# One-hot matrices of a top-k expert layer, written slot-innermost for experts 2 to 7

## What is computed

```python
logits = xf @ router_w + router_b
scores = jax.nn.softmax(logits, axis=-1)
G, idx = jax.lax.top_k(scores.T, K)            # K = 512 of 2048 tokens, for each of 8 experts
toks = xf[idx]
h1 = jax.nn.relu(jnp.einsum('ekh,ehf->ekf', toks, w1) + b1[:, None, :])
eo = jnp.einsum('ekf,efh->ekh', h1, w2) + b2[:, None, :]
y = jnp.zeros_like(xf).at[idx.reshape(-1)].add((eo * G[..., None]).reshape(-1, h))
```

## Time and profile before

| | |
|---|---|
| median of 3 runs | 611.17 us (611.14 to 612.07) |
| the profiled execution | 611.78 us, of which the span is 609.9 us |
| mean granted PE clock | 0.993 of full speed |
| experts' part of the span | 399 to 603 us |

### The profile page before, as it was taken

The page is one execution under the profiler, slowest core; times in us unless marked ns, Lnnn a source line. Parts: engine busy times, 40 slices in busy tenths (PEclk is TensorE's granted clock), DMA queues, the critical chain, the costliest instruction groups (busy, mean ns, idle before and its releaser), DMA issues.

```text
span 609.9 us, 12823 instructions
## 1 busy us (share of the span) xinstructions
PE 564.1 (92%) x5053; PEld 332.2 (54%) x5053; DVE 435.4 (71%) x797; ACT 397.9 (65%) x771; POOL 194.7 (32%) x192
## 2 busy tenths in 40 slices
PE   5899899989999999999999998899999999999991
PEld 4433333334343343433334444479889898898981
DVE  4789879996889968899894257646765757755620
ACT  1677799977988879898888720054655555646641
POOL 4048030043600335100194020230633625427324
PEclk9999999999999999999999999999999999999997
DMA  8600000001000000000000150012634645346123
GB/s 277 229 1 1 1 1 3 2 1 37 2 35 2 2 36 1 37 1 2 36 35 2 37 172 2 27 46 101 139 103 105 164 123 130 108 105 163 18 25 34
DMA packets 23759, 35.76 MB, mean 59 GB/s; under 512 B 3443, under 2 KB 16148, under 8 KB 23572
## 3 DMA queue, kind: packets, MB, share of 16 engines
q1 hardware_dynamic: 17556, 26.56, 13.2%
q0 software_dynamic: 6144, 8.39, 8.0%
HBM read 26.56 MB, written 8.39 MB: 57 GB/s over the span
## 4 chain that ended last, share of the span: by engine, by line
PE 68%; DVE 17%; ACT 5%; issue 4%; POOL 3%; DMA 1%; SPq 0%; POOLq 0%; ACTq 0%; DVEq 0%
PE ps L1578 15%; PE ps L1571 15%; PE ps L1363 11%; DVE mquart L958 11%; PE ps L1350 6%; PE ps L1329 5%; PE ps L1265 3%; ACT probs L703 2%; PE ps L1241 2%; POOL xn L500 2%; PE ps L1387 1%; PE ps L1405 1%; PE ps L1418 1%; PE ps L1540 1%; PE ps L1549 1%
## 5 line engine op out<-in xcount | busy, mean ns | idle before, releaser
L958 DVE TENSOR_REDUCE mquart<-ps 128x2 f32<-128x802 f32 x256 | 241.7, 987 | 34.4 <-PE ps L1329 31.1
L703 ACT ACTIVATE probs<-ps 128x512 f32<-128x512 f32 (+1 forms) x416 | 222.2, 599 | 23.8 <-PE ps L1350 20.9
L1363 PE MATMUL ps<-probs,vp 128*32 128x256 f32 (+1 forms) x1664 | 132.7, 391 | 4.2 <-ACT osb L612 4.2
L1205 DVE TENSOR_TENSOR h1l<-hf,h1h 128x512 fp32r<-128x512 f32 x64 | 44.1, 690 | 70.7 <-ACT hf L815 70.7
L1329 PE MATMUL ps<-kpad,qrows 64*128 64x401 bf16 x512 | 90.0, 337 | 3.7 <-DVE mquart L958 3.1
L1350 PE MATMUL ps<-qfull,kpad 64*128 64x256 bf16 (+1 forms) x832 | 87.9, 272 | 1.8 <-ACT xf L625 0.6
L814 ACT ACTIVATE h1h<-ps,b1T 128x512 fp32r<-128x512 f32 x64 | 43.9, 686 | 61.1 <-PE ps L1571 60.9
L1578 PE MATMUL ps<-w2h,h1h 128*128 128x256 f32 x256 | 73.8, 288 | 1.4 <-DVE h1l L1205 0.7
L1578 PE MATMUL ps<-w2l,h1h 128*128 128x256 f32 x256 | 72.4, 283 | 0.0
L1578 PE MATMUL ps<-w2h,h1l 128*128 128x256 f32 x256 | 72.3, 283 | 0.0
L582 POOL DMA_INDIRECT out<-eo,idx_put x32 | 54.8, 1713 | 29.6 <-ACT eo L824 20.4
(11 more groups left out here) (175 smaller groups left out, 702.3 us busy)
## 6 DMA issues: line engine op xcount, KB each, us to landing
w1raw<-in_L_ffn_w SPq DMA_DIRECT2D x16, 512.0 KB, 4.3
w2raw<-in_L_ffn_w SPq DMA_DIRECT2D x16, 512.0 KB, 4.6
xs<-in_x SPq DMA_DIRECT2D x4, 512.0 KB, 7.5
ctx_sb<-in_ctx SPq DMA_DIRECT2D x3, 512.0 KB, 5.9
out<-xs SPq DMA_DIRECT2D x3, 512.0 KB, 4.5
x_rows<-x SPq DMA_DIRECT2D x3, 512.0 KB, 2.6
b2b<-in_L_ffn_b SPq DMA_DIRECT2D x1, 1024.0 KB, 11.9
out<-xs SPq DMA_DIRECT2D x2, 256.0 KB, 2.0
```

Source lines behind the costliest of these rows:

```text
L703: nc.scalar.activation(out_p, ps[0:w, next_bank(), :], ACT.Exp, scale=float(SCALE)).then_inc(s_ex, 1)
L958: nc.vector.tensor_reduce(mquart[:, u % 2, t, a, :, kq], ps[:, b:b + 2, 0:MAXW], AX.X, ALU.max).then_inc(s_mr, 1)
L1205: nc.vector.tensor_tensor(h1l[:, f, :], hf[:, f % 2, :], h1h[:, f, :].bitcast(F32), ALU.subtract).then_inc(s_hl, 1)
L1363: last = mm(ps[32 * hh:32 * hh + 32, PV, 0:UW], vp[0:w, kt, g, hh, :], probs[0:w, step % PROBS, hh, :], start=(kt == 0), stop=(kt == NKT - 1))
```

## The change

The tile `onehot` gets a second view, `by_tile` [128 partitions, 16 tokens t, 128 slots r], over the same memory. The one-hots of experts 0 and 1 are written and read as before. Those of experts 2 to 7 are written through `by_tile`: the compare takes `iota_b`, repeated over t, against `pos_row` with each value repeated over 128 slots. `fill_slots` loads `by_tile[:, t, :]`, 128 contiguous bf16, where it loaded `onehot[:, :, t]`, 128 values with a step of 16 elements (32 bytes). The count of instructions, the element counts, the semaphores and the order on every engine stay.

```diff
+FIRST_SLOTS = 2
...
+        by_tile = onehot[:, :, :].rearrange("p r t -> p (r t)").rearrange("p (t r) -> p t r", r=P)
...
-                nc.vector.tensor_tensor(onehot[:, :, a:a + NT], iota_x[:, :, a:a + NT],
-                                        pos_row[:, n:n + NT].unsqueeze(1).to_broadcast([P, P, NT]), ALU.is_equal).then_inc(s_oh, 1)
+                if e < FIRST_SLOTS:
+                    out, row = onehot[:, :, a:a + NT], iota_x[:, :, a:a + NT]
+                    pos = pos_row[:, n:n + NT].unsqueeze(1).to_broadcast([P, P, NT])
+                else:
+                    out, row = by_tile[:, a:a + NT, :], iota_b[:, :].unsqueeze(1).to_broadcast([P, NT, P])
+                    pos = pos_row[:, n:n + NT].unsqueeze(2).to_broadcast([P, NT, P])
+                nc.vector.tensor_tensor(out, row, pos, ALU.is_equal).then_inc(s_oh, 1)
...
-                    last = mm(ps[:, 0, 0:5 * NT], onehot[:, :, t], dat_hit[:, t, :, :].rearrange("p s j -> p (s j)"),
+                    last = mm(ps[:, 0, 0:5 * NT], onehot[:, :, t] if e < FIRST_SLOTS else by_tile[:, t, :], dat_hit[:, t, :, :].rearrange("p s j -> p (s j)"),
```

## The result

| | before | after |
|---|---|---|
| median, runs side by side | 611.61 us (6 runs) | 607.74 us (6 runs) |
| ratio | | 0.994, 95% interval 0.9926 to 0.9954 |
| the profiled execution, its span | 611.78, 609.9 us | 608.77, 606.9 us |
| one expert's period (experts 1 to 5) | 24.94 to 24.96 us | 24.34 to 24.35 us |

The changed kernel is 3.9 us faster (2.8 to 4.5 by the interval). The forecast was 3.1 us less, 608.1 us. A second set of runs, on the same chip as the last experiments, gave 607.76 us against 611.60, again 0.994.

What follows compares the result with a forecast made beforehand. PE's unbroken chain through each expert was taken as the bound. Six slot fillings 0.52 us shorter gave 3.1 us, with VectorE's extra 6.5 us hidden: 608.1 us from the median 611.17, range 607.4 to 609.6.

Steps and rivals of the forecast that it cites:

- The bound and the ceiling: PE works without a break in the experts; a free slot filling gives at most 1.23 us an expert, 7.4 us in all.
- Part 1: TensorE's slot-filling loads, made contiguous: pairs from 64 to 26 ns, 0.52 us for each expert, 3.1 us in all.
- Five waits may show at 26 ns, 0.05 us off: In the slot filling, five already-met waits between loads may show at the faster pace: 0.05 us deducted from 0.57 us.
- The Trainium skill's two rules: On weight loads: one has strided loads already fast, gain 0; the other has 16-byte lines, bf16 steps free up to 8.
- Part 2: VectorE's 24 one-hot compares of experts 2 to 7 slow from 422 to 692 ns, 6.5 us more work, priced at nothing.
- recorded slack of 1.40 us: Tightest cover for VectorE, `h1l` of step 2 behind two one-hots; gone when one costs over 0.70 us more.
- What is late next: At each expert's head, down waits for `h1l` of step 0; the pattern moves 0.52 us earlier, the wait neither grows nor swallows the gain.
- Sum: Profiled execution 611.78 - 3.1 = 608.7 us; from the median, 611.17 - 3.1 = 608.1 us.
- 1 (issue at 40 to 45 ns): Slot-filling loads get shorter, but issue and waits hold the pair's pace: gain 1.8 us, 609.4 us; chance 0.07.
- 2 (the step is not the cause): Strided slot-filling load is slow for another reason and stays at 64 ns a pair: 611.2 us; chance 0.05.
- 3 (the compare as slow as `gteq`): One-hots at 4.8 ns per element, about 2.5 us each, become the bound (threshold about 1.1 us): about 631 us; chance 0.03.
- 4 (another chain sets the period): An engine not tied to up step 7 (weights' DMA, POOL's scatters) sets the 24.95 us period: 611 us; chance 0.02.

Runs made afterwards that it cites:

- e1: Kernel before with only the slow compare in experts 2 to 7 (4-byte position operand), strided weight loads kept: ratio 1.0009, 611.71 us against 611.33.
- e7: Changed kernel with each one-hot of experts 2 to 7 written twice: 613.06 us, 5.3 us over the changed kernel.
- e8: Changed kernel with each one-hot of experts 2 to 7 written three times: 620.42 us, 12.7 us over the changed kernel (single run).
- e9: Changed kernel with VectorE's slots(e+2) moved from ahead of the four biased adds to behind them: 606.13 us against 607.76 for the changed kernel.
- e2: Kernel before with contiguous weight loads only, in experts 2 to 7; one-hots written as before, expert 1's row list reused: 607.93 us, ratio 0.9943.
- e3: Kernel before with only expert 1's row list reused and sums in unused columns, strided loads kept, as a control: ratio 1.000.
- e4: Kernel before with the 16 slot matmuls of experts 2 to 7 left out, expert 1's row list reused: 605.03 us against 611.33, ratio 0.9904.
- the sweep: Kernel before plus groups of 16 load-and-matmul pairs at several steps and column counts; repeated with 512-column matmuls between: 25 ns a pair at step 1, 60 at 16.
- e6: Changed kernel with experts 0 and 1 in the new layout too: 608.81 us, ratio 0.9956, 1.1 us over the changed kernel.

## Why the prediction was right, point by point

- **The bound and the ceiling.** PE without a break in the experts: right. The ceiling of 1.23 us for each expert was read from two windows that also differ at their ends; leaving the work out gave 1.11 us.
- **Part 1.** Right in mechanism, a little small in size. The term was 0.52 us for each expert and measured 0.61; six of them are 3.7 us, in agreement with the 3.9 us between the medians. Two steps of it were off. "Five waits may show at 26 ns, 0.05 us off": they do not (only three of them stand between loads, one for each further group of four). The pair itself was right: in the changed kernel the 16 matmuls cover 0.56 us with 0.17 us for one, 26 ns each, so the pairs give the 0.57 us of the sum. The other 0.04 us come from the step into the up matmuls, which I had left as it is: it went from 0.06 to 0.02 us. 0.57 + 0.04 = 0.61.
- **The Trainium skill's two rules.** Rows 4 already showed 168 ns against 96. The fast load "packed or strided", of the Trainium skill's page "TensorE: Matmul & The Clock Gate", section "Weight-path perf modes", does not describe the pace here: step 16 costs 60 ns and more. Of the Trainium skill's page "SBUF — State Buffer", section "SBUF: two separate sides", the 16-byte line is right, and so, nearly, is what that section says of two hits in a line being needed for full bandwidth: step 4, with two, costs 33 ns. The figure in that section of the Trainium skill, 8 bf16 elements as a free step, does not hold here: step 8 costs 60 ns.
- **Part 2.** 692 ns were forecast, 684 measured, 6.3 us more DVE work in all, at no cost; `e1` shows it alone. The end taken from the two rows on one line was the right one. The place where the slack was read to end was right too (`h1l` of step 2), but its size was not: 0.54 us were left where the reading gives 0.86. 0.28 us of the difference is the cast `w2h` ahead of it, which takes 0.69 us instead of 0.41 (last section); I had priced the compare alone and no neighbour of it. So the totals of `e7` (5 us forecast, 5.3 measured) are partly luck. From the recorded slack of 1.40 us, two one-hots of 0.95 us more each make `h1l` 1.9 - 1.4 = 0.5 us late, 2.5 us in five experts; the 1 us an expert that was expected there does not follow from it. `e8` (12 to 14 forecast, 12.7 measured) is the same case: 2.4 us an expert expected, 1.9 by the recorded slack, 2.7 measured.
- **What is late next.** Right: the wait at the head neither grew nor took the gain. I had read this wait only as harmless; that 0.4 us of DVE work in its way was worth 1.6 to 2.0 us I saw later.
- **Sum.** The profiled execution came out at 608.77 us where 608.7 was forecast, and this agreement is partly luck: its experts gave 3.7 us, and 0.6 us went ahead of them. The first up step starts at 400.45 us, and at 399.84 in the profile of before. The difference arises in the gather of expert 0's rows. Its first instruction on POOL takes 1.47 us, and 1.23 us in the profile of before. That is not chance: it is 1.47 us in five profiles (both of the changed kernel, `e7`, `e8`, `e9`) and 1.23 us in the five of before, `e1`, `e2`, `e3` and `e4`. So the changed kernel pays 0.24 us here, which nothing in the prediction foresaw. VectorE's four one-hots of expert 1 lie beside that instruction and take 1.43 us where they took 1.50 to 1.52. The cause stays open, as experts 0 and 1 are computed as before. Most of the rest (4.04 us against 3.73 until the last rows had landed) belongs to the single execution: it is 3.77 us in the repeated profile of the changed kernel.
- **Rivals.** 1 (issue at 40 to 45 ns): the pace is 26 ns. 2 (the step is not the cause): excluded by the sweep. 3 (the compare as slow as `gteq`): it has 1.3 ns for each element, not 4.8; its mechanism is real beyond the threshold. 4 (another chain sets the period): excluded by `e4`.

## What to carry to other kernels

For bf16 weights of 128 columns, a load-and-matmul pair cost about 0.5 ns for each 16-byte line that the load touches, and never less than 25 ns. Where the moving operand is short (20 or 56 columns here), lay the tile out so that the loaded index is innermost, or at a step of at most 3 bf16; at 128 moving columns it was worth only 56 against 62 ns. A layout change moves cost from one engine to another: make it where the engine that pays has slack, and leave it where that engine is on the chain (experts 0 and 1 here). After a gain on the bounding engine, read the small waits left on its chain; what runs ahead of them on another engine, and could as well run behind, is cheap to move.

## What the runs showed that I had not expected

- The granted clock fell from 1.00 to 0.50 of full speed (2.4 to 1.2 GHz) at about 420.6 us in the first sweep, although the profile has PE 100% busy there. Since 417.05 us PE had run nothing but pairs of 20 moving columns and a few matmuls of 256. The clock came back near 424 us, while PE ran the group with 128 moving columns. With 512-column matmuls between the groups it stayed at 1.00, and in the changed kernel 0.4 us of such pairs at a time did nothing to it.
- The cast `w2h` behind the second `h1l` became slower in the changed kernel, as in `e1` and `e6`: 0.69 to 0.71 us in experts 1 to 5, where it took 0.41 to 0.42 (1.4 us in all, hidden). It lies beside a scatter of POOL in both kernels. Before, it starts 0.33 us after the scatter, and the scatter takes 1.89 us:

```profile
455.55 1.89 POOL L582 DMA_INDIRECT out<-eo,idx_put  x1 [0.30 <-issue]
...
455.88 0.41 DVE L1016 CAST w2h<-w2raw 128x512 fp32r<-128x512 f32 x1
```

  After, it starts 0.65 us behind the scatter, and now the scatter takes 1.61 us and the cast 0.69:

```profile
454.96 1.61 POOL L584 DMA_INDIRECT out<-eo,idx_put  x1 [0.30 <-issue]
...
455.61 0.69 DVE L1018 CAST w2h<-w2raw 128x512 fp32r<-128x512 f32 x1
```

  The same 0.28 us has passed from one engine to the other, and the other experts from 1 to 5 look alike (scatter 1.89 to 1.96 us before, 1.61 to 1.64 after). That one waits for the other is my reading; no run takes the two apart.

- In the profiled execution of the changed kernel ACT starts `h1h` of step 3 about 1.2 us late in experts 1 to 6 (457.80 us, with its up step done at 456.55), at no cost to PE. The second profile of the same program has no such pause, and neither has `e1`, `e2` or `e9`; but the profile of `e6` has it again (0.4 to 1.1 us), in expert 6 too, whose loop has no one-hots, and so has `e7`. It comes and goes between executions; its cause stays open.
